# Expert weights loaded in halves between token gathers, a pause behind each of the last eleven gathers, and the fifth expert split in twelve parts

## The reference

```python
x = layernorm(x + wave_attention(x))          # projections, convolution along the sequence, output projection
x = layernorm(x + fp4_ffn(x))                 # weights and rows quantised to 4 bit in blocks of 16
x = layernorm(x + window_attention(x))        # windows of 128 rows
x = layernorm(x + moe(x))

def moe(x):                                   # T = 4096 rows, 8 experts, top 2
    w, idx = top_k(softmax(x @ Wr), 2); w = w / (w.sum() + 1e-20)
    out_all = (silu(x @ Wg[e]) * (x @ Wu[e])) @ Wd[e]   # for each expert e, hidden width 512
    out = sum over the two chosen experts of w * out_all[e, row]
    return out + (silu(x @ Sg) * (x @ Su)) @ Sd          # a shared expert
```

## Time and profile before

| | |
|---|---|
| timed runs, us | 1072.73, 1067.34, 1070.17 (median 1070.17) |
| profiled execution, us | 1075.23 (its span 1073.4) |
| busy, us of the span | TensorE 1012.1, VectorE 765.9, ScalarE 498.0, POOL 446.8 |
| mean granted TensorE clock | 0.984 |
| DMA in all | 88.21 MB, mean 82 GB/s; POOL's queue 35.66 MB |

### The profile page before, as it was taken

One profiled execution on the slowest core, in us unless ns is written; L12 is line 12 of the kernel. 1 busy time (PEld: TensorE's weight loads), 2 busy tenths in 40 slices (PEclk: granted clock), 3 DMA queues, 4 the chain that ended last, 5 costly groups with the idle time before them and its releaser, 6 DMA issues.

```text
span 1073.4 us, 18367 instructions
## 1 busy us (share of the span) xinstructions
PE 1012.1 (94%) x5960; PEld 895.1 (83%) x5960; DVE 765.9 (71%) x1288; ACT 498.0 (46%) x914; POOL 446.8 (42%) x447
## 2 busy tenths in 40 slices
PE   6889997799999999999999899999999999999994
PEld 5667777699999998999987788887889888888883
DVE  7999998999999987788779344444444444446986
ACT  7736855765544444676751133232333333333326
POOL 1001220546554446333100688885662200028886
PEclk9989998999999999999999999999999999999997
DMA  8210000000100000311160456566333111224335
GB/s 310 77 40 20 1 30 0 1 2 0 34 0 0 0 2 1 123 41 40 40 236 1 152 173 207 196 195 189 114 113 114 55 55 56 75 63 122 105 108 196
DMA packets 41378, 88.21 MB, mean 82 GB/s; under 512 B 5970, under 2 KB 27732, under 8 KB 39892
## 3 DMA queue, kind: packets, MB, share of 16 engines
q0 software_dynamic: 9696, 35.66, 10.7%
q1 hardware_dynamic: 20804, 39.20, 10.2%
q10 hardware_dynamic: 10800, 12.32, 3.7%
HBM read 57.80 MB, written 29.36 MB: 81 GB/s over the span
## 4 chain that ended last, share of the span: by engine, by line
PE 49%; DVE 26%; DVEq 9%; POOL 8%; issue 4%; ACT 2%; DMA 1%; another core or an unknown queue 1%; ACTq 0%; POOLq 0%
PE PS L1849 13%; PE PS L1851 13%; PE PS L1850 12%; POOL gathered L1049 6%; PE PS L2252 3%; PE PS L2004 2%; DVE qsc L1285 2%; DVE hx L1302 2%; DVEq L1453 2%; DVE hx L1300 2%; DVEq L1301 2%; POOL pause L1053 1%; PE PS L2236 1%; DVE hv L1430 1%; DVE qinv L1291 1%
## 5 line engine op out<-in xcount | busy, mean ns | idle before, releaser
L1789 DVE TENSOR_TENSOR hb<-PS,gs 128x512 f32<-128x512 f32 x71 | 49.1, 692 | 106.0 <-PE PS L1851 94.6
L1049 POOL DMA_INDIRECT gathered<-expert_outputs,pos x64 | 66.8, 1044 | 132.6 <-DMA expert_outputs<-ye 120.4
L1849 PE MATMUL PS<-EWs,xeh 128*128 x284 | 118.7, 418 | 3.3 <-issue 2.8
L1851 PE MATMUL PS<-EWs,xel 128*128 x284 | 111.3, 392 | 0.0
L1850 PE MATMUL PS<-EWs,xeh 128*128 x284 | 111.1, 391 | 0.0
L1849 PE MATMUL PS<-WGh,bxh 128*128 128x352 f32 x256 | 87.4, 341 | 12.2 <-DVE hv L1430 9.1
L791 ACT ACTIVATE heh<-PS 128x512 fp32r<-128x512 f32 x71 | 42.5, 599 | 112.5 <-PE PS L2252 96.2
L2004 PE MATMUL PS<-WD,htf 128*128 128x256 f32 x384 | 88.5, 380 | 1.6 <-ACT htf L577 1.5
L1849 PE MATMUL PS<-EWs,heh 128*128 x284 | 85.3, 300 | 2.3 <-issue 1.5
L1851 PE MATMUL PS<-WGh,bxl 128*128 128x352 f32 x256 | 84.8, 331 | 0.0
L1850 PE MATMUL PS<-WGl,bxh 128*128 128x352 f32 x256 | 84.7, 331 | 0.0
(11 more groups left out here) (386 smaller groups left out, 3060.1 us busy)
## 6 DMA issues: line engine op xcount, KB each, us to landing
raw_of<-experts POOLq DMA_DIRECT2D x6, 1536.0 KB
expert_outputs<-ye SPq DMA_DIRECT2D x71, 128.0 KB
xe<-tokens_by_expert ACTq DMA_DIRECT2D x65, 128.0 KB
xraw<-xT SPq DMA_DIRECT2D x8, 512.0 KB, 4.0
X<-x SPq DMA_DIRECT2D x1, 4096.0 KB, 13.2
tokens<-X SPq DMA_DIRECT2D x8, 512.0 KB, 3.0
y<-X SPq DMA_DIRECT2D x7, 512.0 KB
raw_of<-experts SPq DMA_DIRECT2D x2, 1536.0 KB, 9.0
```

Source lines behind the costliest of these rows:

```text
L1049: pool.indirect_dma_start(out=gathered[c][:, j, t], out_offset=None, in_=YS, in_offset=bass.IndirectOffsetOnAxis(ap=pos[:, j, 4 * c + t:4 ...
L1789: dve.tensor_tensor(hb[:, h], PS[:, 3], gs[:, h], ALU.mult).then_inc(e_hb, 1)
L1849: pe.matmul(out_, wh, vh, start=first, stop=False)
L1851: return pe.matmul(out_, wl, vh, start=False, stop=last_)
```

## The change

- Each expert load becomes two DMAs of 768 KB (PIECES = 2) with a semaphore each. The wait for a half stands in `split_part`, ahead of parts 0 and 6.
- Expert 2's halves are issued behind the first and the third gather of group 1, and expert 3's behind the first and the third gather of group 9. The waits for a whole load ahead of groups 2 and 10 go.
- Behind each of the 11 gathers of groups 14 to 16 POOL drains and adds 128x256 zeros.
- Expert 4 is split in the twelve parts, without a drain.
- Experts 5 to 7 are loaded in halves, issued one behind the other, and split as wholes as before.
- One semaphore of the last layer norm (`d_ln_last`) is merged into `d_ln`.

```diff
+PIECES = 2
+PIECE = EW // PIECES
-        d_raw2 = sem("d_raw_on")
+        d_raw2 = [sem("d_raw_on" + str(n)) for n in range(PIECES)]
...
             def split_part(e, n):
...
+                if n % (PARTS // PIECES) == 0:
+                    pool.wait_ge(d_raw2[n // (PARTS // PIECES)], 16 * (e - 1))
                 if half == 0:
...
-            def gather_tokens(first, end, split=None, part=0, every_=2):
+            def gather_tokens(first, end, split=None, part=0, every_=2, load=None, pace=False):
...
                         fetch(stages[g % STAGES][:, n], i, d_stage[g % 2])
+                        if pace:
+                            pool.drain()
+                            pool.tensor_tensor(ohr[:], zrow[:], zrow[:], ALU.add)
+                        if load is not None and n % 2 == 0:
+                            load_piece(load, n // 2)
...
+            def place_freed(e):
+                used = pool.value_load(cum_tiles[0:1, e - SLOTS:e - SLOTS + 1], min_val=1, max_val=NE)
+                pool.wait_ge(e_dn, used)
+                pool.tensor_tensor(freed[:], zrow[:, 0:4], zrow[:, 0:4], ALU.add)
+
+            def load_piece(e, n):
+                cols = slice(n * PIECE, (n + 1) * PIECE)
+                pool.dma_start(raw_of[(e + 2) % SLOTS][:, cols], experts[e][:, cols]).then_inc(d_raw2[n], 16)
+
             def load_expert(e):
...
-                pool.dma_start(raw_of[(e + 2) % SLOTS][:], experts[e]).then_inc(d_raw2, 16)
+                place_freed(e)
+                for n in range(PIECES):
+                    load_piece(e, n)
...
-            load_expert(2)
-            gather_tokens(0, 2)
+            gather_tokens(0, 1)
+            gather_tokens(1, 2, load=2)
             pool.wait_ge(d_dn, 2 * AHEAD)
-            pool.wait_ge(d_raw2, 16)
             gather_tokens(2, 8, split=2)
             gather_tokens(8, 9)
-            load_expert(3)
-            gather_tokens(9, 10)
-            pool.wait_ge(d_raw2, 16 * 2)
+            place_freed(3)
+            gather_tokens(9, 10, load=3)
             gather_tokens(10, 12, split=3, every_=1)
             gather_tokens(12, 14, split=3, part=8)
-            gather_tokens(14, len(GROUPS))
-            load_expert(4)
+            gather_tokens(14, len(GROUPS), pace=True)
+            place_freed(4)
+            for n in range(PIECES):
+                load_piece(4, n)
             keep(len(GROUPS) - 1)
-            loaded(4)
+            for n in range(PARTS):
+                split_part(4, n)
```

More of the change, by code:

```diff
@@ L295, in build @@
         d_gr = [sem("d_gathered" + str(i)) for i in range(NCH)]
-        d_gr_last, d_mv_last, d_rs_last, d_ln_last = (sem("d_" + n + "_last") for n in ("gr", "mv", "rs", "ln"))
+        d_gr_last, d_mv_last, d_rs_last = (sem("d_" + n + "_last") for n in ("gr", "mv", "rs"))
         x_kept, d_tile, d_row, d_table, d_token_of, d_stage0, d_stage1, d_rows, d_row0, d_row1, d_last = (
@@ L402, in _ @@
             sp.wait_ge(d_last, 1)
-            sp.wait_ge(d_ln_last, 1)
+            sp.wait_ge(d_ln, NCH + 1)
             sp.dma_start(out[:, bass.ds(4 * NCH - 2, 2)], X[:, bass.ds(4 * NCH - 2, 2)]).then_inc(s_out, 16)
@@ L828, in _ @@
             at = 4 * (NCH - 1) + 2
-            act.activation(X[:, at], X[:, at], ACT.Identity, scale=rstd4[:, NCH - 1, 2:3], bias=nmr4[:, NCH - 1, 2:3]).then_inc(d_ln_last, 1)
+            act.activation(X[:, at], X[:, at], ACT.Identity, scale=rstd4[:, NCH - 1, 2:3], bias=nmr4[:, NCH - 1, 2:3]).then_inc(d_ln, 1)
         @block.gpsimd
@@ L1008, in gather_tokens @@
                         keep(g - 1)
-            def load_expert(e):
[L1011 to L1014, removed]
-                pool.dma_start(raw_of[(e + 2) % SLOTS][:], experts[e]).then_inc(d_raw2, 16)
+            def place_freed(e):
[5 more added lines that the diff above has]
+                pool.dma_start(raw_of[(e + 2) % SLOTS][:, cols], experts[e][:, cols]).then_inc(d_raw2[n], 16)
+            def load_expert(e):
+                place_freed(e)
+                for n in range(PIECES):
+                    load_piece(e, n)
             def loaded(e):
-                pool.wait_ge(d_raw2, 16 * (e - 1))
+                for n in range(PIECES):
+                    pool.wait_ge(d_raw2[n], 16 * (e - 1))
                 split_expert(e)
```

## The result

The changed kernel takes 1103.59 us (median of four runs, 1099.82 to 1105.94), the kernel before beside it 1070.56: the ratio is 1.0302, with a 95% interval of 1.028 to 1.0325. The forecast was 1067.5 with a range up to 1074, so it was wrong, and its rival C, a drain that waits for the gather, came in with its place; that its 1104 was met so closely is in part luck, as the part on the prediction shows. Where a few executions of a kernel ran some per cent longer at a lower granted clock, they are left out of its median and its ratio. The profiled execution took 1099.82 us, its span is 1098.0.

What follows compares the result with a forecast made beforehand. It took TensorE, busy 1012.1 of 1073.4 us, as the bound, so POOL matters only where it stalls TensorE. Of 2.2 + 4.2 = 6.4 us won, a 3.7 us wait leaves 2.7: 1070.17 - 2.7 = 1067.5 us, range 1060.5 to 1074.

Steps and rivals of the forecast that it cites:

- rival C: Chance 0.10: the pause is dearer; drains waiting for gathers make 37 us, expert 4 ready at 797.5, kernel 1104 us.
- (b): Pauses behind the 11 gathers of groups 14 to 16: drain 0.15, +0.75 us each, +8.25 in all; 4.2 us regained.
- The addition: The 128x256 addition on POOL in each pause of groups 14 to 16, put at 0.74 us.
- the step from gather to gather: On POOL in the last three groups, a gather was to come every 2.0 us instead of every 1.3.
- (d): At tile 32, TensorE arrives at 756.8, expert 4's weights at 760.5: new wait of 3.7 us, leaving 2.7 of 6.4.
- (a): Loads of experts 2 and 3 in halves between gathers: POOL some 2.65 us ahead, no stall at expert 3's first tile.
- The 2.2 us that I took: Gain at tiles 2, 14 and 15 from the loads in halves, half of the 4.45 us lost there; bounds 0 and 4.45.
- the gain term of 4.2 us for tiles 24 to 26: The pause between the last 11 gathers was to win back 4.2 us lost at these tiles; bounds 0 to 4.2.
- The cause by density of gathers: TensorE's lost time in three stretches fits POOL's runs of 8, 8 and 11 gathers without tensor operations between.
- (c): Expert 4's load and split on POOL: start +5.6 us, 3.16 us wait gone, twelve parts 17.4 us, ready at about 760.5.
- The rule of the Trainium skill: Batch transfers to at least 1 MiB; if it held for load 4, expert 4's weights come 2 us later, median 1069.5.

Runs made afterwards that it cites:

- the doubled addition: The changed kernel without drains, with two additions kept apart by a semaphore in each pause: 1079.13 us, ratio 1.001 to the kernel before.
- the version with expert 4 first: The changed kernel with expert 4 loaded ahead of group 14, its split parts as the gathers' pauses, no drain or idle addition: ratio 0.9926, again 0.9936.

## Why the prediction was wrong, point by point

- **The step that failed is the drain in (b): "The drain's bounds: 0, and the 3.52 us ... so I stay near those."** I took 0.15 us each, 1.7 for the eleven, and they cost 31.1. The bounds held the mean of 2.8 us; single ones went beyond, with 6.54 and 3.69. I chose the value from drains that had tensor operations ahead of them and no fresh DMA, and the drain in question stood directly behind a DMA. The nearest row by its neighbour would have been a landing, not a gap between tensor operations; the landing alone takes 1.8 to 3.9 us there. I had that reading as rival C and gave it one chance in ten.
- **C's 1104 was in part luck.** It had 37 us of drains and expert 4 ready at 797.5; measured were 31.1 and 785.45, 12 us earlier. By C's own rule (each us behind 763.23 is a us of the kernel) 785.45 gives 22.2 us, about 1092, and with the 2.7 us of the lower clock about 1095. The two profiles do lie that far apart (24.6 us). The medians lie 33 us apart, because the executions profiled stood 4.7 over and 3.8 us under their medians, which C had not priced.
- **The addition** was 0.61 to 0.63 us, not 0.74, and the step from gather to gather without the drain 1.78 us, not 2.0.
- **The place was right, and the slope nearly.** (d) said that expert 4's weights and tile 32 move towards each other and that each further us of POOL is a us of the kernel. POOL was ready 785.45 - 760.5 = 25.0 us later than forecast; TensorE waited 30.5 instead of 3.7. With the doubled addition 7.9 us more on POOL gave 5.7 us more of waiting, and 8.2 us with the clock behind it. The drains put behind expert 4 cost 5.6 instead of 33. Not in the sum was the lower clock after the wait, 2.7 us.
- **(a), the halves:** POOL no longer waits for expert 3 (0.30 us idle ahead of the first gather of group 10, at 672.54, instead of 3.66), no stall at tile 23, as forecast. The 2.2 us that I took, half of 4.45 without a row behind it, are near the 1.4 and 2.2 us of the two ratios, of which one interval includes 1. That they come from tiles 2, 14 and 15 isn't shown: on one chip the kernel before and the halves alone lose the same there, and on another tile 2 loses 2.1 us less with the halves.
- **(b), the gain term of 4.2 us for tiles 24 to 26** is 0.1 us in one further profile of the kernel before and 2.5 in another. The profiled execution was 5 us over the median; I carried that over to the median as if it had nothing to do with the lost tiles. The cause by density of gathers fits, but isn't proven: in all eleven profiles in which something stood between these gathers, tiles 24 to 26 lost at most 0.7 us, and of the seven without it three lost 2.5 to 4.2 and four at most 0.3. So density doesn't suffice for the loss, and what else it takes is not known. In the kernel after, tiles 24 to 26 are 4.83 to 4.88 us apart, and the idle time of ScalarE that was 3.66 us in the earlier trace rows is 1.47.
- **(c):** the split in twelve parts took 770.10 to 785.45, 15.4 us, against 17.4: 1.28 us from part to part, nothing for the semaphore. Its first half was awaited until 6.4 us behind the issue: POOL stood idle 2.70 us for it, where I had said that the wait of 3.16 would go.
- **The rule of the Trainium skill** (DMA: Bandwidth & Descriptors, Measured), to batch transfers to at least 1 MiB, didn't show as a cost of the halves here. By the fit on the same page of the Trainium skill (Anatomy of one DMA — SWDGE (gpsimd) path), about 2.0 us + bytes / 436e3, the estimate was 7.6 us for two halves in turn and 5.6 for a whole. The first half of load 4 was in use 6.4 us behind the issue, and no half landed later than 8.1 us behind its own, so that the second, issued at about 764.3, was there by 772.4 and no part waited for it; the whole was in use 10.4 us behind its issue in the earlier trace rows. Other transfers were under way beside both, so this doesn't measure the fit.

## What to carry over

Price a drain by what stands ahead of it on its engine: behind a gather it costs as much as waiting for that gather to land, even if everywhere else in the profile it is nearly free. When an engine is slowed down on purpose, first find what is queued behind the slow stretch and how much room it has; the same eleven pauses cost 33 us in front of the fifth expert's load and some 6 behind it, and useful work (the parts of the split) spaces the gathers as well as idle work does. And before losses read from one profile are counted as a gain, profile the same kernel again: if the execution was 5 us over the median, some of them may be that.

## What the runs showed of the hardware

- A drain of POOL behind an indirect DMA of 128 KB took 1.9 to 4.0 us in three kernels, and 6.4 to 7.9 us where it was the first of the row; waiting for the landing of such gathers took 1.8 to 3.9 us. Behind tensor operations with one old DMA a drain took 0.23 us.
- POOL's first drain behind all the gathers took 3.5 to 3.8 us, with the last gather 19 to 41 us old, but 1.8 us in the version with expert 4 first. With one drain ahead of it in the run of gathers it took 4.3 or 1.6 us. It is not known what it counts.
- Eleven gathers issued every 1.25 us went with a loss of 2.5 to 4.2 us of TensorE in three profiles and of at most 0.3 in four; every 1.78 us or slower, tiles 24 to 26 lost at most 0.7 us in all profiles of this study.
- After 30.5 us in which TensorE had nothing to do the granted clock was at 0.50, and 0.81 on the mean of the 14 us that followed, with products at 0.63 us instead of 0.39. Short waits had it too: tiles that waited 4.1, 4.3 and 7.2 us lost 5.8, 5.9 and 9.9 us, with the clock at 0.50 behind the wait, while one that waited 1.5 us lost 1.7 at a clock of 1.00.
